# Issuing a filter load ahead of two other transfers on one DMA queue

## What is computed

```python
def _L0_xattn_ref(k, v, q, ssm_kernel, D, head_dim):   # head_dim = 8, k = v = context
    kv = jnp.einsum('bhil,bhjl->bijhl', k_, v_)         # products of pairs of rows in a head
    kv_f = jnp.fft.rfft(kv, n=fft_size)
    kernel_f = jnp.fft.rfft(ssm_kernel, n=fft_size)     # one filter of length 1024 for each head
    y = jnp.fft.irfft(kv_f * kernel_f, n=fft_size)[..., :L]
    out = y + kv * D[None, None, None, :, None]
    out = jnp.einsum('bijhl,bhil->bjhl', out, q_)
...
x = x + jnp.tanh(g_xattn[0]) * _L0_xattn_ref(ctx, ctx, _layernorm(x), L0_xattn_ssm_kernel, L0_xattn_D, 8)
x = x + jnp.tanh(g_ffn[0]) * _L0_ffn_ref(_layernorm(x), ...)    # gate, 7 routed experts, 1 shared
```

## Time and profile before

| | us |
|---|---|
| median of 3 runs | 4265.64 (4265.6 to 4265.89) |
| the profiled execution | 4265.89 |
| its span, first to last instruction | 4264.1 |
| the convolution stage in it | about 40 to 1950 |
| PE busy over the span | 4125.0 (97%) |
| DVE busy over the span | 2600.3 (61%) |

### The profile page before, as it was taken

One profiled execution on the slowest core, in us unless ns is written; L12 is line 12 of the kernel. 1 busy time (PEld: TensorE's weight loads), 2 busy tenths in 40 slices (PEclk: granted clock), 3 DMA queues, 4 the chain that ended last, 5 costly groups with the idle time before them and its releaser, 6 DMA issues.

```text
span 4264.1 us, 71266 instructions
## 1 busy us (share of the span) xinstructions
PE 4125.0 (97%) x25930; PEld 3759.3 (88%) x25930; DVE 2600.3 (61%) x2980; ACT 1890.9 (44%) x2451; POOL 987.7 (23%) x1200
## 2 busy tenths in 40 slices
PE   6999999999999999996899999999999999999998
PEld 6999999999999999995788788888898888988986
DVE  5999999999999999995343432222223323323331
ACT  6787777777778777772111111111112212212120
POOL 1333233332333323230000024540011111211111
PEclk9999999999999999997999999999999999999999
DMA  7888988889888898887223234233433433443332
GB/s 168 223 217 212 222 212 220 217 213 221 213 218 218 212 222 212 220 211 126 87 74 104 87 92 129 75 113 97 119 95 97 114 76 97 95 99 99 83 93 47
DMA packets 280375, 634.14 MB, mean 149 GB/s; under 512 B 45840, under 2 KB 111866, under 8 KB 280246
## 3 DMA queue, kind: packets, MB, share of 16 engines
q1 hardware_dynamic: 218582, 413.89, 33.9%
q0 software_dynamic: 61664, 218.41, 26.6%
HBM read 311.03 MB, written 170.16 MB: 113 GB/s over the span
## 4 chain that ended last, share of the span: by engine, by line
PE 49%; DMA 2%; DVE 1%; issue 1%; ACT 0%; SPq 0%; POOL 0%; DVEq 0%; POOLq 0%; ACTq 0%
PE moe_ps L1654 11%; PE moe_ps L1655 11%; PE moe_ps L1656 11%; PE moe_ps L1672 5%; PE moe_ps L1674 5%; PE moe_ps L1673 5%; PE moe_psT L1643 1%; DMA out<-moe_y,moe_add_i 1%; DMA moe_y<-out 1%; DVE moe_zl L1552 1%; DMA out<-moe_y 0%; ACT moe_zh L1324 0%; DVE moe_hid L1565 0%; DVE moe_y L1579 0%; DMA moe_zin<-zT_d 0%
## 5 line engine op out<-in xcount | busy, mean ns | idle before, releaser
L1654 PE MATMUL moe_ps<-moe_zh,moe_w1h 128*128 128x512 f32 (+2 forms) x2368 | 861.1, 364 | 36.6 <-DVE moe_zl L1552 22.1
L1655 PE MATMUL moe_ps<-moe_zl,moe_w1h 128*128 128x512 f32 (+2 forms) x2368 | 859.0, 363 | 0.0
L1656 PE MATMUL moe_ps<-moe_zh,moe_w1l 128*128 128x512 f32 (+2 forms) x2368 | 856.6, 362 | 0.0
L693 PE MATMUL att_psY<-att_kv_hi,att_tz_hi 128*128 128x288 f32 x2560 | 775.4, 303 | 51.4 <-DMA att_kv_lo<-att_kv 43.6
L695 PE MATMUL att_psY<-att_kv_hi,att_tz_lo 128*128 128x288 f32 x2560 | 755.7, 295 | 0.0
L694 PE MATMUL att_psY<-att_kv_lo,att_tz_hi 128*128 128x288 f32 x2560 | 755.5, 295 | 0.0
L1565 DVE TENSOR_TENSOR moe_hid<-moe_ps,moe_act_s 128x512 f32<-128x512 f32 (+2 forms) x148 | 91.6, 619 | 890.1 <-PE moe_ps L1656 871.4
L693 PEld LDWEIGHTS att_psY<-att_kv_hi,att_tz_hi 128*128 128x128 f32 x2560 | 481.6, 188 | 68.4 <-issue 57.8
L1654 PEld LDWEIGHTS moe_ps<-moe_zh,moe_w1h 128*128 128x128 f32 x2368 | 446.0, 188 | 89.2 <-issue 38.1
L1656 PEld LDWEIGHTS moe_ps<-moe_zh,moe_w1l 128*128 128x128 f32 x2368 | 447.7, 189 | 51.3
L1655 PEld LDWEIGHTS moe_ps<-moe_zl,moe_w1h 128*128 128x128 f32 x2368 | 446.5, 189 | 50.6 <-issue 0.2
(11 more groups left out here) (188 smaller groups left out, 7926.9 us busy)
## 6 DMA issues: line engine op xcount, KB each, us to landing
att_kv_lo<-att_kv POOLq DMA_DIRECT2D x128, 1152.0 KB, 12.3
att_kT<-in_cT SPq DMA_DIRECT2D x64, 512.0 KB, 11.6
att_xn<-in_x SPq DMA_DIRECT2D x64, 512.0 KB, 5.8
out<-att_x SPq DMA_DIRECT2D x64, 512.0 KB, 4.0
z_d<-att_z SPq DMA_DIRECT2D x64, 512.0 KB, 9.0
zT_d<-att_zT SPq DMA_DIRECT2D x64, 512.0 KB, 5.3
moe_zin<-zT_d SPq DMA_DIRECT2D x64, 512.0 KB, 4.9
moe_y<-out SPq DMA_DIRECT2D x128, 256.0 KB, 4.3
```

Of the source, the lines that this page charges most:

```text
L693: nc.tensor.matmul(acc, w_hi[:, cols], x_hi, start=start, stop=False, skip_group_check=True)
L1654: nc.tensor.matmul(acc, w1h[:, c, cols], zh[:, c, 0:w], start=(c == 0), stop=False)
L1655: nc.tensor.matmul(acc, w1h[:, c, cols], zl[:, c, 0:w], start=False, stop=False)
L1656: last = nc.tensor.matmul(acc, w1l[:, c, cols], zh[:, c, 0:w], start=False, stop=(c == C - 1))
```

## The change

In `step` of the SP program, `load_filter` of the next head stands first. It stood behind `load_keys` of the head after the next and `store_zT` of the head before the last. Nothing else is different.

```diff
             def step(h, u, ahead, back, back2):
+                if ahead:
+                    load_filter(h + 1, 1 - u)
                 if not (isinstance(h, int) and h >= H - 2):
                     load_keys(h + 2)
                 if back2:
                     store_zT(h - 2)
-                if ahead:
-                    load_filter(h + 1, 1 - u)
                 if back:
                     store_x1(h - 1)
                 if ahead:
```

## The result

| | us |
|---|---|
| changed kernel, median | 4329.51 (4325.57 to 4335.59) |
| kernel before, median beside it | 4265.77 |
| ratio, 95% interval | 1.0147 (1.013 to 1.0165) |
| the profiled execution, its span | 4343.53, 4341.7 |

The changed kernel is 64 us slower; the forecast was no change. It is the rival of the other side, the longer critical transfer, at more than three times the price that I gave it.

A forecast was written before the change was run, and what follows sets the result against it. DVE was taken to set the pace at 29.67 us a step, PE right behind. On the profiled 4265.9: + 1.0 - 1.5 + 0 = 4265.4, with the median 0.25 lower, 4265; range 4256 to 4274.

The forecast's parts named there:

- the rival of the other side: Second half of kv_lo lands 0.45 us later each step, PE starts block 4 later: 20 us, 4286; chance 0.11.
- DVE sets the pace and the filter had 12.5 us to spare: Convolution's steady part: DVE's 29.67 us a step unshortened, filter landing 12.5 us before its user; gain 0.
- When the filter goes out, and that the keys are in time: SP's queue: filter issued 8.1 us earlier, keys about 2.4 us later, landing near 1033 with nearly 5 us cover; cost nothing.
- The critical transfer: Second half of kv_lo, before block 4: last 128 packets meet filter instead of keys, 0.45 us less each step.
- The bound on the other side: Second half of kv_lo: filter packets cost at most as much as z's, 4.86 us, 0.45 us more.
- What a longer transfer costs: PE at block 4: delay beyond 0.12 us slack a step recurs each step; 0.45 us gives 61 x 0.33 = 20 us.
- The start: Steps 0 and 1: first kv_lo transfer slowed, + 1.0 us; block 4's stop in step 1 shortened, - 1.5 us.

The follow-up runs named there:

- the parts' losses: Changed kernel with one filter part from separate rows: only the low part overlapping, 48 us (1.0113); only the high part overlapping, 36 us (1.0081).

## Why the prediction was wrong

*DVE sets the pace and the filter had 12.5 us to spare: right.* One more DVE instruction cost 31 us, half of the add left out won 4.5, with no change in its interval, and no run showed an engine waiting for the filter.

*When the filter goes out, and that the keys are in time: right.* The filter went out as the step began, the keys 3.2 us behind it, not 2.4, since SP stood 2.47 us in the issue of the low part. Their landing cost nothing: no engine waited for them in 160 to 1880 us.

*The critical transfer: the step that failed.* The prediction took the add's time from mean rates: "what counts is how long the neighbour's packet is", and from the earlier trace rows "a transfer that is 0.45 us shorter". The rates were right: after 11.5 us 250 packets of the add had been sent, 249 before. But a transfer lands with its last small packet, and a mean rate does not show that tail. In the tail the filter, read from overlapping rows, goes at 0.32 MB in 2 us in place of 0.65 from separate ones. The add's data is all sent as early as before (12.3 us in the median, 12.5 before), but its small packets come late: it lands after 14.3 us in the median, not 13.0 or less. The bound on the other side was wrong for the same reason. I had taken the slowest neighbour's mean rate, + 0.45 us, and 1.35 us came. The rows gave a sign of it: at the mean rates of the earlier trace rows the 256 packets, which begin some 2 us after the issue, are sent 11.3 us after it, and the add landed at 13.5. Those 2 us of tail are where the loss arose, and the working had no term for them. What in the engines holds the small packets back is not shown. (The Trainium skill, DMA: Bandwidth & Descriptors, Why a DMA increments its semaphore by 16 and not by 1, says that the engines of one DMA finish independently and each counts the semaphore up once, behind its own data; by that rule the slowest engine sets the landing. The trace agrees as far as it goes: 16 packets of 4 bytes in each add, and a landing about 0.3 us after the last of them.)

*What a longer transfer costs: right in form.* The rival had 0.12 us of slack a step and the rest in full. With the medians of the add that is (14.3 - 13.0 - 0.12) x 61, or 75 us with the 1.35 us taken exactly, and the two profiled executions, from which these medians are, lie 77.6 us apart. In part that is luck. The fifty steps at the full clock grew by 30.7 - 29.7 = 1.1 us, not by 1.2, and 14 us came from the seven steps in which the clock fell, for which the working had no term. The rival's 20 us came from its 0.45 us, not from its mechanism.

*The start: right in sign, wrong in size.* The first add took 8.9 us as before (+ 1.0 forecast; the first matmul starts at 39.95, before at 40.01), and the L570 with which the earlier trace rows begin comes at 150.78, 3.5 us earlier (- 1.5 forecast).

## What to carry to other kernels

Moving a transfer forward is only free if nothing critical is in flight at its new place; the spare time of the moved transfer says nothing about that. For a transfer at the edge, don't work with the mean packet rate alone, but look at what the engines send when most of its data is through, since it has landed only when the last of its small packets is. And where two engines are both near full, the cheap test is one that makes each of them a bit longer.

## What the runs showed of the hardware

128 rows of 3072 bytes that overlap within 3.6 KB of HBM (or within 5 KB, 16 bytes apart) are read much more slowly than separate ones when the other queue has hardly anything to send: 117 packets in 2 us against 225 in the transfers shown, 124 against 218 in the medians. While the add had packets beside them, the two made no difference to it (250 and 254 packets of the add in 11.5 us). In the kernels with overlapping rows there, the add's last data packet and its landing lie 1.3 to 1.6 us apart in place of 0.5.

In the changed kernel a stop of PE of 1.7 to 2.1 us at block 4 was followed seven times by a granted clock of 0.50 (1.2 GHz) for 3.4 us, some ten times not. A step with it took 2.1 us more than the others.

Whether it is a bank of HBM that all engines ask at once was only argued. It is open, too, why the overlapping load did little harm behind the keys (1.001), where it was also sent with no add beside it, and why the parts' losses, 48 and 36 us, sum to more than the whole.
